# Order of the prologue, of GpSimd's queue and of a table load in a kernel of four attention layers and an expert layer

## What is computed

```python
h = x                                   # x: layer-normalized input
for l in range(4):
    xn = _ln(h, ln1_w[l], ln1_b[l])
    h = h + _attn(xn, Wq[l], bq[l], Wk[l], bk[l], Wv[l], bv[l], Wo[l], bo[l], u_bias[l])
    fn = _ln(h, ln2_w[l], ln2_b[l])
    h = h + gelu(fn @ W1[l].T + b1[l]) @ W2[l].T + b2[l]
...
# _attn
scores = jnp.einsum('bhqd,bhkd->bhqk', q, k)
rel = jnp.einsum('bhqd,ld->bhql', q + u[None, :, None, :], r)
scores = (scores + _rel_shift(rel, S, S)) * HEAD_DIM ** (-0.5)   # causal mask, softmax, @ v
...
# experts, on the normalized sum
scores = jax.nn.sigmoid(xf @ router_w.T)            # 16 experts in 4 groups, best 2 groups, best 4
shared_out = jax.nn.silu(sg) * su @ shared_down_w.T
h = jax.nn.silu(g) * u                              # per expert, 32 wide
routed = jnp.einsum('esh,ehc->sc', h * combine, down_w)
return (shared_out + routed).reshape(B, T, C)       # added to the sum
```

## Time and profile before

| | |
|---|---|
| median of 3 runs | 2445.75 us (2442.41 to 2451.73) |
| the profiled execution | 2444.17 us, of which the span in the trace 2442.2 us |
| busy, TensorE matmul | 2298.7 us, 94% of the span |
| busy, TensorE weight load | 1976.5 us, 81% (beside the matmuls) |
| busy, VectorE | 2052.2 us, 84% |
| busy, ScalarE | 1828.2 us, 75% |
| busy, GpSimd | 1145.8 us, 47% |
| last residual of the layers, first product of the experts | 2082.52 and 2103.58 us |

### The profile page before, as it was taken

One profiled execution on the slowest core, in us unless ns is written; L12 is line 12 of the kernel. 1 busy time (PEld: TensorE's weight loads), 2 busy tenths in 40 slices (PEclk: granted clock), 3 DMA queues, 4 the chain that ended last, 5 costly groups with the idle time before them and its releaser, 6 DMA issues. The chain is left out here.

```text
span 2442.2 us, 83077 instructions
## 1 busy us (share of the span) xinstructions
PE 2298.7 (94%) x31360; PEld 1976.5 (81%) x31360; DVE 2052.2 (84%) x5069; ACT 1828.2 (75%) x2837; POOL 1145.8 (47%) x2091
## 2 busy tenths in 40 slices
PE   2799999999999999999999999999999998599998
PEld 1688888888888888888888888888888887477776
DVE  3899999898888989898898989888888984577774
ACT  2488887888888888888888888888888887455554
POOL 4455555554545445555545555555545442233332
PEclk9899999999999999999999999999999999799999
DMA  6332333333333333333333333333333330100000
GB/s 178 90 87 81 88 89 90 91 90 90 86 89 89 92 87 90 86 90 89 91 90 95 90 91 90 90 91 91 90 89 86 91 85 15 43 27 27 27 23 18
DMA packets 221142, 196.03 MB, mean 80 GB/s; under 512 B 28880, under 2 KB 217424, under 8 KB 220752
## 3 DMA queue, kind: packets, MB, share of 16 engines
q1 hardware_dynamic: 220752, 190.73, 27.8%
HBM read 14.46 MB, written 4.19 MB: 8 GB/s over the span
## 5 line engine op out<-in xcount | busy, mean ns | idle before, releaser
L898 DVE TENSOR_REDUCE rowmax<-bank 128x4 f32<-128x1024 f32 (+1 forms) x768 | 914.8, 1219 | 113.8 <-PE bank L498 101.9
L708 ACT ACTIVATE probs<-bank 128x1024 f32<-128x1024 f32 x768 | 745.1, 1024 | 96.2 <-PE bank L555 83.9
L555 PE MATMUL bank<-qstack,kstack 64*128 64x128 f32 (+1 forms) x4096 | 433.8, 304 | 0.0
L498 PE MATMUL bank<-kstack,qstack 62*128 62x256 f32 (+1 forms) x4096 | 426.9, 305 | 0.0
L749 ACT ACT_TABLE_LOAD x256 | 328.4, 1283 | 4.6
L1001 POOL TENSOR_SCALAR ve<-mv 128x2 f32<-128x2 f32 x256 | 56.6, 221 | 557.8 <-DVE mv L838 546.2
L498 PEld LDWEIGHTS bank<-kstack,qstack 62*128 62x128 f32 x4096 | 315.5, 193 | 0.0
L555 PEld LDWEIGHTS bank<-qstack,kstack 64*128 64x128 f32 x4096 | 314.7, 191 | 0.0
L544 PE MATMUL bank<-maskT_half,pick_half 64*128 64x128 bf16 (+1 forms) x3072 | 268.9, 241 | 14.4 <-DVE turn_c L867 6.9
L640 PE MATMUL bank<-w,hidden 128*128 128x128 f32 x2048 | 270.0, 275 | 2.6 <-ACT hidden L758 2.6
L487 PE MATMUL bank<-mask_half,pick_half 64*128 64x128 bf16 (+1 forms) x3072 | 269.8, 243 | 2.7 <-DVE rowmax L898 1.4
(11 more groups left out here) (144 smaller groups left out, 5283.7 us busy)
## 6 DMA issues: line engine op xcount, KB each, us to landing
qstack<-base SPq DMA_DIRECT2D x768, 128.0 KB, 2.4
kstack<-base SPq DMA_DIRECT2D x384, 128.0 KB, 2.4
turn_x<-turn_c SPq DMA_DIRECT2D x512, 32.0 KB, 1.8
qstack<-maxrows SPq DMA_DIRECT2D x256, 16.0 KB
xin<-in_x SPq DMA_DIRECT2D x16, 256.0 KB, 3.1
out<-ot SPq DMA_DIRECT2D x16, 256.0 KB, 2.4
h_all<-in_x SPq DMA_DIRECT2D x2, 512.0 KB, 6.0
w<-in_w SPq DMA_DIRECT2D x4, 256.0 KB, 3.2
```

The costliest lines, as they stand in the source:

```text
L498: last = pe.matmul(bank[:, b0 + b, i * wide:(i + 1) * wide], qstack[rows, r, p0 + i, t * 128:(t + 1) * 128], kstack[rows, r, p0 + i, 0:wid ...
L555: last = pe.matmul(bank[:, b0 + b, i * wide:(i + 1) * wide], kstack[rows, r, p0 + i, kt * 128:(kt + 1) * 128], qstack[rows, r, p0 + i, q0: ...
L708: act.activation(probs[:, k], bank[:, A_BANK[k]:A_BANK[k] + 2, :], ACT.Exp, scale=SCALE).then_inc(exp_done[k], 1)
L898: dve.tensor_reduce(rowmax[:, n % 2, t, :, p0:p0 + heads], bank[:, M_BANK[k]:M_BANK[k] + 2, :].rearrange("p b (h c) -> p b h c", h=heads), ...
```

## The change

It has four parts.

1. **Prologue.** SP loads x in six pieces instead of five (the first has two batches instead of four) and in another order, behind four semaphores instead of two. VectorE clears two quarters of qstack and GpSimd the other two, both ahead of all else. VectorE's second pair of batches, the masks' casts and the sum of the biases move behind apply_1 of batch 0. ScalarE places the keys of two quarters ahead of slot 0 and of two behind split_first of batches 0 and 1. TensorE starts with the eye and ln_cols landed, and waits for the masks at s = 1.
2. **Slots of the layers.** GpSimd's xn1_split(s+1) stands ahead of turned(s); VectorE's turn_cosines(s) stands ahead of apply_1(s+1) and of apply_0 and stats_0. SP waits for the keys quarter by quarter.
3. **Experts, first group.** Its tiles and semaphores are made ahead of both blocks (`Early`). Five loads are issued by SP in slot 112. VectorE computes group 0's residual and statistics behind slot 131 and the norm behind slot 132, GpSimd the power behind slot 131. The expert block loads only w_down and x of group 1, and TensorE waits for VectorE's split of w_in ahead of the first product instead of ahead of everything.
4. **Experts, tables.** ScalarE computes the score at u = 1 between half_out(., 0) and half_out(., 1) instead of behind both. A one-column sigmoid stands ahead of half_out(., 0), a one-column silu behind the score; each brings its table.

```diff
-X_STARTS = (0, 4, 8, 16, 24)
+X_STARTS = (0, 2, 4, 8, 16, 24)
...
@@ SP, layers
             rows_of_x(0)
-            sp.dma_start(staged[:, 0:6 * 128], a["c_halves"]).then_inc(squares_landed, 16)
-            sp.dma_start(eye, a["c_eye"]).then_inc(squares_landed, 16)
-            sp.dma_start(w_qkv[:, 0], a["w_qkv"][0]).then_inc(consts_landed, 16)
...
+            sp.dma_start(w_qkv[:, 0], a["w_qkv"][0]).then_inc(w0_landed, 16)
+            sp.dma_start(eye, a["c_eye"]).then_inc(first_landed, 16)
...
+            sp.dma_start(staged[:, 0:6 * 128], a["c_halves"]).then_inc(halves_landed, 16)
             sp.dma_start(turn[:], a["c_turn"].rearrange("p (a n) -> p a n", a=2)).then_inc(consts_landed, 16)
+            rows_of_x(1)
             sp.dma_start(b_v[:], on_all("b_v")).then_inc(consts_landed, 16)
-            rows_of_x(1)
+            rows_of_x(2)
...
-            sp.wait_ge(keys_placed, RING)
+            def experts_early():
+                sp.dma_start(ex.w_in[:], a["w_in"]).then_inc(ex.landed, 16)
+                sp.dma_start(ex.w_router[:], a["router"]).then_inc(ex.landed, 16)
...
+                sp.dma_start(ex.x0[:].rearrange("p (b t) d -> p b t d", b=GT // T), x_tiles[:, 0:GT // T]
+                             ).then_inc(ex.landed, 16)
@@ content
-                sp.wait_ge(stack_cleared, min(n + 1, RING))
+                sp.wait_ge(stack_cleared, RING)
+                sp.wait_ge(keys_placed, min(n + 1, RING))
@@ slots of SP
                 if live(s):
                     exchange(s)
+                if s == N - B // 2:
+                    experts_early()
@@ VectorE, layers
             dve.memset(expo[:], -0.5).then_inc(expo_filled, 1)
+            for r in (2, 3):
+                dve.memset(qstack[:, r].bitcast(F32), 0.0).then_inc(stack_cleared, 1)
...
             stats_0(0)
-            dve.wait_ge(squares_landed, 48)
-            dve.tensor_copy(pick_half[:], picks_f).then_inc(consts_cast, 1)
             apply_0(0)
-            stats_0(1)
-            cast_masks(0)
-            apply_0(1)
...
             for s in SLOTS:
                 if live(s + 1):
                     stats_1(s + 1)
+                if s == -1:
+                    stats_0(1)
...
+                if live(s):
+                    turn_cosines(s)
                 if live(s + 1):
                     apply_1(s + 1)
+                if s == -1:
+                    dve.wait_ge(halves_landed, 16)
+                    dve.tensor_copy(pick_half[:], picks_f).then_inc(consts_cast, 1)
+                    cast_masks(0)
+                    cast_masks(1)
+                    apply_0(1)
...
-                if live(s):
-                    turn_cosines(s)
...
+                if s == N + 3:
+                    experts_stats()
+                if s == N + 4:
+                    experts_norm()
@@ GpSimd, layers
+            clear_stack(0)
+            clear_stack(1)
             pool.wait_ge(expo_filled, 1)
             power_0(0)
-            power_0(1)
-            pool.wait_ge(consts_landed, 16 * CONST_DMAS)
+            pool.wait_ge(w0_landed, 16)
             split_qkv(0)
             for s in SLOTS:
-                if live(s):
-                    xn1_split(s)
...
+                if live(s + 1):
+                    xn1_split(s + 1)
                 if live(s):
                     turned(s)
                 if s == -1:
-                    clear_stack(0)
+                    power_0(1)
+                    power_0(2)
                 if s == 0:
-                    clear_stack(1)
                     prefill()
                 if s == 1:
-                    clear_stack(2)
-                    clear_stack(3)
                     split_w1(0)
...
+                if s == N + 3:
+                    pool.wait_ge(ex.mv_ready, 1)
+                    pool.tensor_scalar(ex.ve[:], ex.mv[:, :, 1], 1e-5, None, ALU.add).then_inc(ex.ve_ready, 1)
+                    pool.wait_ge(ex.ve_ready, 1)
+                    pool.tensor_tensor(ex.rstd[:], ex.ve[:], expo[:, 0:GT], ALU.pow).then_inc(ex.rstd_ready, 1)
@@ SP, experts
-            sp.dma_start(eye[:], a["c_eye"]).then_inc(weights_landed, 16)
+            sp.dma_start(w_down[:], a["w_down"].rearrange("(c p) n -> p c n", p=128)).then_inc(weights_landed, 16)
...
-            load(0, 0)
             load(1, 1)
@@ TensorE, experts
-            pe.wait_ge(weights_landed, 16 * WEIGHT_DMAS)
-            pe.wait_ge(weights_split, 2)
+            pe.wait_ge(ex.landed, 16 * EX_DMAS)
...
+                if n == 0 and i == 0:
+                    pe.wait_ge(weights_split, 2)
@@ ScalarE, experts
+            def load_table(count, function):
+                at_least(act, etables_loaded, count)
+                act.activation(table_probe[:], expo[:, 0:1], function).then_inc(etables_loaded, 1)
...
+                    if u == 1 and live(q + 1):
+                        load_table(2 * (q + 1), ACT.Sigmoid)
                     if live_tile(n - 2):
                         half_out(n - 2, 0)
+                    if u == 1 and live(q + 1):
+                        act.wait_ge(logits_done, q + 2)
+                        at_least(act, combine_ready, q + 1)
+                        act.activation(score[:].rearrange("p t e -> p (t e)"), bank[:, 6, 0:GT * E], ACT.Sigmoid
+                                       ).then_inc(score_ready, 1)
+                        load_table(2 * (q + 1) + 1, ACT.Silu)
...
                     if live_tile(n - 2):
                         half_out(n - 2, 1)
...
-                    if u == 1 and live(q + 1):
-                        act.wait_ge(logits_done, q + 2)
...
```

More of the change, by code:

```diff
@@ L27 @@
 from contextlib import ExitStack
+from dataclasses import dataclass
 import numpy as np
@@ L77 @@
 GU = E * EH + HS
+GT = 4
+EX_DMAS = 5
 HIGH, LOW = 3.0e38, -3.0e38
@@ L160, in position_tables, with early_parts, sb, sem @@
     return {"c_turn": turn.reshape(128, -1), "c_keys": keys, "c_eye": eye, "c_halves": halves}
-def layers_program(nc, a, h_all):
+@dataclass
+class Early:
+    w_in: object
+    w_router: object
+    bias_rows: object
+    eye: object
+    x0: object
+    stats: object
+    mv: object
+    ve: object
+    rstd: object
+    xn: object
+    landed: object
+    x1_ready: object
+    stats_done: object
+    mv_ready: object
+    ve_ready: object
+    rstd_ready: object
+    xn_ready: object
+def early_parts(nc, ctx):
+    def sb(name, shape, dt=F32):
+        return ctx.enter_context(nc.sbuf_tensor(name, shape, dt))
+    def sem(name):
+        return ctx.enter_context(nc.semaphore(name))
+    return Early(
+        w_in=sb("w_in", [128, 2 * GU]), w_router=sb("w_router", [128, E]),
+        bias_rows=sb("bias_rows", [128, E]), eye=sb("eeye", [128, 128]), x0=sb("x0", [128, GT, D]),
+        stats=sb("estats", [128, GT, 6]), mv=sb("emv", [128, GT, 2]), ve=sb("eve", [128, GT]),
+        rstd=sb("erstd", [128, GT]), xn=sb("exn", [128, GT, D]),
+        landed=sem("early_landed"),
+        x1_ready=sem("x1_ready"), stats_done=sem("estats_done"), mv_ready=sem("emv_ready"),
+        ve_ready=sem("eve_ready"), rstd_ready=sem("erstd_ready"), xn_ready=sem("exn_ready"))
+def layers_program(nc, a, h_all, ex):
     with ExitStack() as ctx:
```

107 lines of the change are left out of this document (55 added, 52 removed).

## The result

The changed kernel takes 2415.4 us (median of 4 runs, 2412.9 to 2418.7), the kernel before 2448.4 (4 runs, 2442.4 to 2451.7): a ratio of 0.9874, with a 95% interval of 0.9855 to 0.9893. That is 33 us less, where 39.6 were forecast; 2406 was forecast, with a range of 2391 to 2420. Against the 2445.75 on which the forecast stood, and against the 2445.0 to 2447.1 that the kernel before took beside the later runs, it is some 30 us less.

What follows compares the result with a forecast made beforehand. TensorE, busy 1533 of 1543 us, was taken to bound the layers, leaving small holes. Start 15, layers 4.2, drain -2.9, junction 14 and tables 9.3 sum to 39.6 won: 2406 us as a median, range 2391 to 2420.

Steps and rivals of the forecast that it cites:

- The floor: Start: SP issues the same bytes of loads before its first exchange, so that goes at about 27.3, however early the cosines are.
- a slot is the loop ...: Start, from batch 1: base, sines and cosines, exchange, content, landing take 11.3 a slot; base of batch 3 at 61.4, won 13.
- 99 slots at 0.066: Layers: without collisions of apply_2 with GpSimd's rotation, slots of 15.466 become 15.40, 6.5 won.
- SP idles for several us in a slot, so 0.5 (0 to 3): Layers: five early expert loads, 2.4 of issue on SP and 1.1 MB on the DMA engines, lose 0.5.
- The 2.9: Drain: GpSimd waits in line for experts_stats, so xn2's split starts at about 2069.75 instead of 2066.85; 2.9 lost.
- rival E: Start comes out at 20 and the clock at the junction doesn't fall, TensorE's pause being shorter: 2398 to 2393, chance 0.12.
- Junction: From last residual to experts' second x_turn: x_turn(1) at 2094.0 instead of 2108.04, 14 won, bounds 12 and 16.5.
- Tables: Expert groups: sigmoid's table loads during ScalarE's wait for h_turn, `down` starts 0.62 earlier in each of 15 groups, 9.3 won.
- Rival A: Start gives only 5, its loop running on DMAs behind with loads or TensorE longer at half clock: 2416, chance 0.14.
- rival B: Layers' collisions only move and the experts' sigmoid gains nothing, another wait standing just behind: 2425, chance 0.08.
- C: Layers: GpSimd's queue behind the new wait exceeds its 0.7 cover in every slot, 73 lost: 2479, chance 0.04.
- D: Expert groups: a switch of tables holds ScalarE for 1.4 more, `down` starts 0.8 later than before: 2427, chance 0.02.

Runs made afterwards that it cites:

- run 1: The changed kernel with SP issuing the five early loads of the experts in slot 129 instead of slot 112: 2411.5 us, ratio 0.9862.
- run 2: The changed kernel with GpSimd's power for experts' group 0 at the end of slot 132 instead of 131, behind xn2_split: 2412.6 us, ratio 0.9864.
- 7: run 1's kernel with the splits of w_1 and w_qkv done in pieces of 128 columns, one in a slot: 2410.4 us, ratio 0.9851.
- run 10: The changed kernel with part 3 undone, early loads and group 0's residual, statistics, power and norm at the expert block's head: 2418.8 us, ratio 0.9887.
- run 5: The changed kernel with VectorE's order undone (turn_cosines behind apply_1, apply_0 and stats_0 again) and GpSimd's kept: 2414.8 us, ratio 0.9866.
- run 4: The changed kernel with GpSimd's order undone (xn1_split behind the previous batch's rotation again) and VectorE's kept: 2449.2 us, ratio 1.0020.
- 6: The changed kernel with x from batch 8 on and the weights of layers 1 to 3 loaded in later slots, behind the first exchange: 2414.1 us, ratio 0.9867.
- run 11: run 9's kernel with idle products: four ahead of up, two ahead of down in slots 132 and 133, eight ahead of the second x_turn: 2398.1 us.
- 12: run 9's kernel with half the idle products of run 11: two ahead of up, one ahead of down, four ahead of the second x_turn: 2391.6 us.
- run 3: The kernel before with part 4 (the experts' tables) alone: 2435.8 us, ratio 0.9962.
- run 9: The changed kernel with edits of run 1, run 2 and 7, later loads of x and weights placed otherwise, group 1's x ahead of w_down: 2395.4 us.

## Why the prediction was right, and where not

The time lies in the range and 9 above the point. The sign and the four sources were right; the sum was 6.6 too large by the medians and 14.3 by the two traces. The steps behind the 14.3:

- **Start: mechanism right, size off.** The floor (loads ahead of the exchange, 27.54) and the release of base by DMA came as forecast. The step "a slot is the loop ..." took 2.4 from issue to landing; behind the 3 MB of loads the stacks landed 3.2 after the last content was issued (34.04 to 37.28). The 15 was 13.0 in the profiled execution, and of the kernels with the same start (changed, 1, 2, 7, 10) the gain at batch 7 was 13.0, 12.1, 7.5, 13.0 and 9.5. They also differ in where the stretches at half clock fall between 50 and 110 us; whether that is the cause of these 5 us was not tried. The forecast knew such a spread only as a bound. The extra 1.75 for the cosines is open: without their move batch 7 comes 3.3 later, which lies within this spread (run 5).
- **Slots: right but for layer 0.** Common slots 15.39, forecast 15.40; boundaries -4.5, forecast -4.8. "99 slots at 0.066" came out as 6.3 in 90 slots (5.4 up to n = 111, 0.9 from 114 on). Layer 0's "I add 3" was 1.2, with the cosines back in their place 3.9 (run 5). What the prediction did not see: the two orders depend on each other. With the cosines moved and GpSimd's order left, the kernel is no faster than before (run 4).
- **Early loads: the size was wrong.** "SP idles for several us in a slot, so 0.5 (0 to 3)" looked at the queue that issues. What counted was the transfers ahead of one content: base 2.4 late, and behind it TensorE at half clock for 6.8. The two slots lost 4.9, outside the bounds (run 1).
- **Drain: the term was right, and the clock was missing.** The 2.9 were measured as 2.7 (run 2), and in runs 1 and 6, where both `down`s ran at the full clock, the drain is 3.2 longer than before. The other 5 of the 7.7 came from TensorE at 1.2 GHz; in the kernel before it was at it for 3.4 us of its drain, in the changed one for 20.5. They are a matter of the execution too, as drains with the same order lasted between 82.9 and 87.4. The prediction carried the clock only as a chance at the junction in rival E, and not in the drain. That the clock falls for TensorE's pauses is likely (runs 11 and 12); that the added wait makes it fall is not shown (runs 1 and 2).
- **Junction: right,** 13.9 for 14, with the second x_turn 11.6 behind the last residual for "about 11", held by the DMA of xin and then by VectorE, as the trace shows. Against a kernel without part 3 but with the other parts 11.8 were won (run 10).
- **Tables: right.** 0.68 a group (run 3), forecast 0.62; the score starts while the copy ends. In the changed kernel's own trace 2 of it went at the head of the experts, where the second x_turn falls into the half clock: from it to the third take 18.53, in the kernel before 16.52 and in run 1 16.44.

Rival A ("only the 5 shown up to batch 1") gave nearly the measured time, but for another reason: the start won 13. Rivals B, C and D are refuted by runs 3 and 5 and by the rows above, though run 4 shows that the collisions of rival B do move when the orders are set differently. Rival E did not come: the start won 13, and the clock fell at the junction for 17 us.

## What to carry to other kernels

Cost a DMA that is moved by what it stands ahead of on the DMA engines, not by its issue: 1.1 MB in a full slot cost 4.9 us, in the drain nothing. When two engines collide in memory, a reordering of one shifts the time of the other; test each order alone before both are called gains. Where TensorE starts to pause, price its products at both clocks, read more than one execution, and try idle products that are shorter than the pause.

## What had not been expected of the hardware

- A cast of 32 columns on VectorE took 0.59 instead of 0.17 when a rotation on GpSimd had begun 0.17 ahead of it (run 4).
- The granted clock stayed at 1.0 through the drain when products that nobody reads filled its pauses (runs 11 and 12). Without them it fell to 0.5 at 2053.5, 5.8 us ahead of the last residual, and stayed there for 20.5 (run 9).
- Each such product of 512 columns in float32 took 0.90 at the full clock (four of them 3.60 in run 11) and not 0.5, and shows as two records (two products: 1.88, x4).
- The same drain, with the same wait of 4.66, had the last two `down`s at 3.75 in the changed kernel and at 2.02 in run 1.
- VectorE clears 2048 float32 columns in 1.76. The Trainium skill (VectorE: DVE Perf Modes, Zero memsets can be issued as uint32) says one cycle per element, which by its clock of 0.96 GHz is 2.1, an estimate; the measurement decides.
